# First stage of an adapter and gated-FFN kernel: eight dense products of the first tile's last chunk moved ahead of its first rank product

## The reference

```python
# layer 0, conditioning (R = 16, SCALING = 2.0)
base_out = jnp.einsum('bti,oi->bto', x, W) + b
A = lora_As[adapter_mapping]
Bm = lora_Bs[adapter_mapping]
lora_h = jnp.einsum('bti,bir->btr', x, A)
lora_out = jnp.einsum('btr,bro->bto', lora_h, Bm)
c = base_out + lora_out * SCALING
# layer 0, feed-forward (D_FF = 1376)
up = c @ W_up.T
gate = silu(c @ W_gate.T)
x = x + (gate * up) @ W_down.T
# layer 1: a dense product plus 8 gated experts of rank 16, twice
x = x + L1_ffn(L1_cond(x))
```

## Time and profile before

| | |
|---|---|
| median of 3 executions | 972.44 us |
| the profiled execution | 973.03 us |
| its span, first to last instruction | 971.3 us |
| TensorE busy (matmul) | 964.6 us, 99% |
| TensorE weight loads | 814.8 us, 84% |
| VectorE busy | 608.0 us, 63% |
| ScalarE busy | 472.6 us, 49% |
| GpSimd busy | 285.7 us, 29% |
| granted TensorE clock | 1.00 |

### The profile page before, as it was taken

How to read it: one execution, slowest core, us unless ns; L and a number is a source line. 1 busy time by engine, 2 the same in 40 slices (tenths; PEclk the granted TensorE clock), 3 DMA queues, 4 the chain that set the end, 5 groups by cost and what they waited for, 6 DMA issues and landing times.

```text
span 971.3 us, 14085 instructions
## 1 busy us (share of the span) xinstructions
PE 964.6 (99%) x4659; PEld 814.8 (84%) x4659; DVE 608.0 (63%) x1027; ACT 472.6 (49%) x877; POOL 285.7 (29%) x380
## 2 busy tenths in 40 slices
PE   8999999999999999999999999999999999999998
PEld 6888888888888888888888888888888999898987
DVE  4795987877973333785332497333378488785871
ACT  4775776664833333671333383333357274535342
POOL 5884225545202511500712220351150460000000
PEclk9999999999999999999999999999999999999999
DMA  7797367786889867877876778986788650616132
GB/s 239 263 343 262 131 241 259 291 289 246 303 267 324 277 194 194 280 265 250 292 248 193 235 233 265 324 280 191 197 292 287 241 194 23 239 46 215 65 109 87
DMA packets 112081, 222.78 MB, mean 229 GB/s; under 512 B 12165, under 2 KB 12166, under 8 KB 111370
## 3 DMA queue, kind: packets, MB, share of 16 engines
q1 hardware_dynamic: 108576, 211.37, 65.2%
q0 software_dynamic: 3296, 10.51, 3.1%
q10 hardware_dynamic: 138, 0.01, 0.0%
HBM read 160.49 MB, written 61.34 MB: 228 GB/s over the span
## 4 chain that ended last, share of the span: by engine, by line
PE 95%; DMA 2%; DVE 1%; ACT 1%; SPq 0%; issue 0%; ACTq 0%
PE bank L2140 95%; DMA x_raw<-in_x 1%; PE bank L2310 1%; DMA t_raw<-t_scratch 1%; SPq L652 0%; DVE xa L1599 0%; ACT c_out L1145 0%; ACT xa L1101 0%; SPq L825 0%; DVE t_lo L1807 0%; ACT t_hi L1307 0%; SPq L828 0%; DVE a_both L1613 0%; DVE hg L1916 0%; DVE lx L1932 0%
## 5 line engine op out<-in xcount | busy, mean ns | idle before, releaser
L2140 PE MATMUL bank<-cop_hi,wring 128*128 128x512 f32 x1234 | 380.5, 389 | 0.0
L2140 PEld LDWEIGHTS bank<-cop_hi,wring 128*128 128x128 f32 x1234 | 231.6, 188 | 48.6 <-ACT bank L1217 0.5
L2140 PE MATMUL bank<-cop_lo,wring 128*128 128x512 f32 x616 | 239.7, 389 | 0.0
L2140 PE MATMUL bank<-op_hi,wring 128*128 128x512 f32 x560 | 173.7, 389 | 0.0
L1744 DVE TENSOR_TENSOR v<-bank,p7s 128x512 f32<-128x512 f32 x44 | 30.4, 692 | 195.2 <-PE bank L2140 195.2
L2140 PEld LDWEIGHTS bank<-cop_lo,wring 128*128 128x128 f32 x616 | 115.6, 188 | 23.9
L2140 PEld LDWEIGHTS bank<-op_hi,wring 128*128 128x128 f32 x560 | 105.1, 188 | 21.8
L2140 PE MATMUL bank<-op_lo,wring 128*128 128x512 f32 x280 | 108.9, 389 | 0.0
L1248 ACT ACTIVATE s<-bank 128x512 f32<-128x512 f32 x44 | 26.3, 597 | 110.7 <-PE bank L2140 110.7
L2140 PE MATMUL bank<-xa,w_hi 128*128 128x512 f32 x256 | 76.3, 392 | 0.5 <-ACT c_out L1145 0.5
L950 POOL TENSOR_TENSOR h_t<-h,h 128x512 f32<-128x512 f32 x20 | 27.1, 1356 | 162.1 <-DVE h L1766 162.1
(11 more groups left out here) (253 smaller groups left out, 1862.4 us busy)
## 6 DMA issues: line engine op xcount, KB each, us to landing
wring<-wgu_scratch SPq DMA_DIRECT2D x231, 256.0 KB, 3.1
wring<-wd_scratch SPq DMA_DIRECT2D x140, 256.0 KB, 5.4
wgu_scratch<-wring SPq DMA_DIRECT2D x77, 256.0 KB, 3.6
xs_raw<-x_scratch SPq DMA_DIRECT2D x16, 512.0 KB, 6.1
out<-res SPq DMA_DIRECT2D x32, 256.0 KB, 2.1
wd_scratch<-dt SPq DMA_DIRECT2D x14, 512.0 KB, 6.0
x_raw<-in_x SPq DMA_DIRECT2D x13, 512.0 KB, 5.3
c_scratch<-c_out POOLq DMA_DIRECT2D x24, 256.0 KB, 5.3
```

The source lines that it names most:

```text
L2140: return e.matmul(out_ap, lhs, rhs, start=start, stop=stop, skip_group_check=True)
```

## The change

For k = 3, tile 0's rank product of group 0 is no longer issued first. It now stands behind eight of tile 0's twelve dense matmuls (four hi x hi and four hi x lo) and ahead of the last four (lo x hi). Tile 1's turn, with tile 0's rank product of group 1 ahead of it, keeps its place. No instruction is added or removed.

```diff
         for k in range(KC):
             for t, ms in ((0, range(KC)), (1, range(KC - 1))):
-                if k == 3:
-                    lora_in(0, (t,))
+                if (k, t) == (3, 1):
+                    lora_in(0, (1,))
                 bank, hi, lo = c_banks(t), xa_hi[t], xa_lo[t]
                 ...
                 e.wait_ge(x_lo, x_n(t, k))
                 for m in ms:
                     mm(bank[m][:, :], w0_hi[:, k, m * P:(m + 1) * P], lo[:, k, :], False, False)
+                if (k, t) == (3, 0):
+                    lora_in(0, (0,))
                 if t == 0:
                     e.wait_ge(w0_lo_done, k + 1)
```

## The result

| | before | changed |
|---|---|---|
| median, measured side by side (8 runs each) | 972.37 us (971.54 to 972.64) | 975.23 us (973.19 to 976.33) |
| the profiled execution | 973.03 us | 973.19 us |
| its span | 971.3 us | 971.4 us |

The ratio is 1.0027, with a 95% interval of 1.0016 to 1.0038. The forecast was 972.5 us, its range ended at 973.4, and "slower" had 0.03. It is wrong. What makes this case worth reading is that the profiled execution, 973.19 us, is the fastest of the eight: it shows just what the prediction said, and the other seven took longer.

A forecast was written before the change was run, and what follows sets the result against it. TensorE, holding 95% of the chain, was taken to bound the kernel; its idle time moves from 20.4 to 24 us, netting +0.05 us. The profiled execution would take 973.08, the median 972.5 us, range 971.5 to 973.4.

The forecast's parts named there:

- Rival A: Second rank product finds its bank free, six matmuls start at 24.82, kernel takes 971.1 us; chance 0.07.
- D: Gap near 20 us has another cause, so the eight moved matmuls wait too; 973.1 us, chance 0.03.
- Rival C: Bank's way through VectorE takes 3.37 us, not 3.09; +0.33, 972.8 us; upper end of the forecast's own case, together 0.88.
- The restart: From the waiting second rank product to tile 1's six matmuls: 1.04 us, or 0.95 if the weight load went ahead.
- No DMA is moved, and SP's and GpSimd's queues keep their times.: Tile 2's loads hang on VectorE's splits of `x`, which the change was said not to delay; no cost counted.
- the old gap: TensorE's idle time near 20.4 us, before the first rank product: 1.20 us by starts, filled by the eight moved matmuls.
- new idle time: TensorE stands from 23.87 to 25.15 before the second rank product, waiting for its bank: 1.28 us of lost starts.
- move with TensorE and give nothing back: Short waits on `c_out` and `lh_lo` follow ScalarE's `h_turned` at 30.80, released by TensorE, so they change nothing.
- Rival B: New idle stretch lets TensorE's clock fall for some 4 us, half of it lost; 974.5 us, chance 0.02.

The follow-up runs named there:

- e1: The changed kernel again, unedited, with a trace of an ordinary execution; median 975.10 us, ratio 1.0023 to the kernel before.
- e13: One more traced execution of the changed kernel, unedited; 975.91 us.
- e4: Changed kernel plus five unused matmuls filling TensorE's idle time before the second rank product; 975.83 us, ratio 1.0025.
- e7: Changed kernel, with GpSimd's first tile 2 copies waiting until tile 1's group 0 has been split; 973.94 us, ratio 1.0011.
- e8: e3's kernel, with GpSimd's first tile 2 copies waiting until tile 1's group 0 has been split; 972.72 us, ratio 1.0002.
- e16: e14's kernel plus a GpSimd write of zeros, 128 columns, behind tile 1's gather to shift the later copies back; 973.71 us, ratio 1.0009.
- e6: The kernel before again, without any edit, for another trace; 972.47 us, ratio 0.9996.
- e9: Kernel before, with GpSimd's first tile 2 copies waiting until tile 1's group 0 has been split; 972.33 us, ratio 0.9996.
- e14: Kernel before, with GpSimd's tile 1 gather moved ahead of its last eight copies; 972.80 us, ratio 0.9998.
- e15: e14's kernel plus a GpSimd write of zeros, 64 columns, behind tile 1's gather to shift the later copies back; 972.93 us, ratio 1.0005.
- e5: Changed kernel, with tile 0's first rank product of chunk 3 behind all twelve dense matmuls; 976.48 us, ratio 1.0039.
- e12: One traced execution of e3's kernel, unedited; 975.96 us.
- e3: Changed kernel, with six of tile 1's dense matmuls of chunk 3 also ahead of tile 0's second rank product; 975.08 us, ratio 1.0023.
- e17: Changed kernel plus a GpSimd write of zeros, 256 columns, between tile 1's gather and the tile 2 copies; 975.58 us, ratio 1.0026.

## Why the prediction was wrong

**What held.** The profiled execution has the eight matmuls at 20.09 (forecast 20.20), the first rank product at 21.90 (22.01), the four `w_lo` at 22.86 (22.96), the second rank product at 25.06 after 1.11 us (25.15, about 1.1), the six at 26.12 (26.19): all within 0.11 us, and from step to step within 0.02. Rival A (the gain comes through) and D (the eight wait as well) are out by the same rows. Rival C, the slow way through VectorE, didn't come: 25.06 - 21.90 = 3.16, against 3.14 with the handoff. The restart took 26.12 - 25.06 = 1.06, so no weight load went ahead of the wait here either. That the whole time came out near 973.08 as well, at 973.19, was luck: it is one execution, the fastest of eight.

**The step that failed: "No DMA is moved, and SP's and GpSimd's queues keep their times."** GpSimd's queue did not keep its times. I followed the rank product's way through ScalarE and VectorE up to L1639 and `lh_lo`, and not the instruction that stands between them, `b_lo` (L1619), for which GpSimd's gathers wait. It is moved later against GpSimd's copies, GpSimd gets through earlier, and its next copies meet L1613. Price, from the six `w_hi` to the third rank product: 31.18 - 25.85 = 5.33 us in e1 and 32.03 - 26.69 = 5.34 in e13, against 29.62 - 26.12 = 3.50 in the first trace of the changed kernel: 1.83. Of four traces of this order (the first, e1, e4, e13) three have it. That it is a cause of the lost time is shown by e7 and e8, which take it away, and by the trace of e16, which has it in the old order. That `b_lo` is the link which brings it about is read from the traces; no run moved `b_lo` alone.

**The size that was off: the old gap as a fixed number.** I set 1.28 us of new idle time against 1.20 of old and got +0.05. But 1.20 was what one execution had. The wait on `a_both`, 1.02 there and 1.03 in e6, was 0.49 in e9, whose edit acts only behind this place:

```profile
20.22 1.22 PE L2140 MATMUL bank<-xa,a_both 128*128 128x256 f32 x8 [0.49 <-DVE a_both L1613]
```

In e16, with TensorE's old order, it was 0.47, and in e14 and e15 there was none. It depends on how early TensorE comes to the rank product against `a_both`, while the new wait is always there (1.10 or 1.11 in each trace). For e1 and e13 I work out where the old order would have stood: operand ready plus 0.05, plus the 26.14 - 21.40 = 4.74 to the six. e1's operand ended at 19.66 + 0.83 = 20.49, which gives 25.28; the six started at 25.85, so +0.57. e13's ended at 21.03, which gives 25.82 against 26.69: +0.87. For the first trace (20.40 + 0.83) it gives 26.02 against 26.12. The lost cover thus costs 0.1 to 0.9 us in these three, by how the two chains lie in the execution; the forecast took the lucky end. This one is worked out from traces, not isolated by a run.

**The small waits "move with TensorE and give nothing back".** The one near 56 us doesn't: ScalarE waits there for a store (2.10 us in the first trace), and TensorE behind it waits 0.25 (first trace), 0.38 (e1), 0.41 (e13), 0.52 (e4) and 0.58 us (e7) there. Neither of the two traces of the kernel before has it. It isn't the changed order's alone, though: e14 and e15, with TensorE's old order and another one on GpSimd, have 0.21 and 0.16.

**The sum.** Against e6, a trace of before with a span of 971.0: the six start 0.07 us earlier in e1 and 0.77 later in e13; the meeting adds 5.33 - 3.50 = 1.83 and 1.84; the wait near 56 us 0.38 and 0.41. That is 2.14 and 3.02, and the spans are longer by 2.1 and 3.2. So the profiled executions are accounted for, save 0.2 us.

**Rival B, the clock.** Not the cause: e4 has no idle time there and is as slow, and the granted clock is 1.00 in the traces of the changed kernel. The mechanism exists all the same: e5's clock fell behind 2.04 us of idle time. How near the changed kernel is to it isn't known, since e12's didn't behind 2.84. The prediction read a lower clock at the start out of matmuls 0.45 us apart; the profile's granted clock is 1.00 there, too, so that reading rests on the spacing alone. In e5 a spacing of (29.95 - 27.39) / 6 = 0.43 stands beside a granted clock of 0.50.

**What stays open.** e3 had three executions of 977.34, 977.90 and 978.41 us, none of which was traced; they went with the meeting (e8 has none), but its price in e12 accounts for 975.96 only. Their mean granted clocks are 0.998, 0.997 and 0.996, like e5's 0.998, and 1.000 in e12. So the clock probably fell behind their wait, and not behind e12's; without a trace this is not shown. It doesn't explain the changed kernel's executions above 976, the highest of which, 977.12, has 1.000; why they exceed 976 stays open. One execution of the kernel before, beside e14, took 976.33 at 0.998, so there the clock may fall, too.

**The method's mistake.** The chance of 0.96 for "same" rested on one execution of before. The sum was right for one execution of after, the fastest, and I had no term for what varies from one to the next.

## What to carry to other kernels

When a step is moved on the bounding engine, follow every instruction that stands behind the one which it releases, on every engine, and ask which two streams now hang on the same event: streams that were apart by chance can be made to start in the same moment, each time anew. Read a wait that is to be hidden as a range, since its size depends on the phase of two chains that start from different loads, and hold it against a second trace before calling it covered. And where the profiled execution lies at the edge of its kernel's times, as here at 973.19 with a median of 975.23, take another trace before explaining anything.

## What the runs showed of the hardware that was not expected

**A VectorE instruction starved by back-to-back copies on GpSimd.** A `tensor_tensor` of 128x256 with both inputs in SBUF (L1613) takes 0.42 to 0.45 us as a rule. When it and GpSimd's run of 128x64 copies begin within 0.02 us of each other, it takes 2.66 or 2.67 (e1, e4, e13; e17 on the second of the pair) or 2.48 and 2.49 (e12, e16). In e1 thirteen copies start in the meantime, 0.18 us from one start to the next as if nothing ran beside them, and only the fourteenth, at 30.35, is slowed, to 0.44 us; in e12 and e16 it is twelve. Where the starts lay 0.16 us (e14) or more apart, with either one first, the pair took 0.82 or 0.83, and most copies beside it 0.42 each: then both engines are slowed and neither stands. No run had a distance in between. So a shift of less than 0.2 us can move an execution of one kernel from one side to the other.

The traces of e1, e4, e12 and e13 have one thing more: L1639, the instruction ahead of L1613, took 0.53 to 0.55 us in place of 0.42, and so held L1613 back by some 0.12 us. Without that, e1's L1613 would have begun about 0.13 us ahead of the copies. What held L1639 isn't shown; at 0.42 it would have ended at 27.99, before the first copy's recorded start, and e16 has the meeting with an L1639 (L1642 there) of 0.43.

The Trainium skill, page "SBUF — State Buffer", section "Who interferes with whom", says that a VectorE instruction with two SBUF inputs contends with a GpSimd instruction that reads SBUF, that the one that issues first has the shared ports for the whole instruction, and that the other fully blocks. The traces agree on who contends; by that rule L1613 would have lost one copy, an estimate of some 0.25 us from e1's row, and it lost 2.25. Why one instruction lets thirteen copies pass in a tie, and is only slowed at 0.16 us of distance, no run here tells. That it is the ports at all is not shown by itself; what is shown is that the meeting of these two does it.

**The reverse is milder.** The 32 copies take 8.38 to 8.40 us when `b_lo` doesn't run among them (e1, e7, e13) and 9.72 when it does (e6): 1.3 us in all. By the traces it was this delay that kept the kernel before clear of the meeting.

**A clock that falls in one trace and not in another.** Waits of 1.1 us and 1.7 us (e1) left the granted clock at 1.00. Behind 2.04 us without a matmul (e5) it went to 0.50, and it was back at 0.98 in the window from 30 to 32 us; behind 2.84 us (e12) it stayed at 1.00. What decides between the last two, no run here tells.
